# A windowed-attention layer with its projections issued as two 64-column matmuls each

## The chip, the cores and the metric

One core of a Trainium2 chip runs the whole kernel. The metric is the device time of one execution in microseconds (us), the median of a few runs; the profile is of one further execution. The engines are named as the profile names them: PE (TensorE, with PEld for its weight loads), DVE (VectorE), ACT (ScalarE), POOL (GpSimd), SP (SyncE, which here issues the DMAs).

## What is computed

The input is x, 16 images of 56 x 56 positions with 384 channels, fp32. It is group-normalised (32 groups), then goes through shifted-window attention with 7 x 7 windows (49 tokens) and 12 heads of 32, and is added to x:

```python
xn = _gn(x)                                    # 32 groups per image
xr = jnp.roll(xn, shift=(-3, -3), axis=(1, 2))
q, k, v = jnp.split(xr @ w_qkv.T, 3, axis=-1)  # cut in 7x7 windows, 12 heads
dots = einsum('bhwid,bhwjd->bhwij', q, k) * 32 ** -0.5
dots = dots + pos_emb[rel[:, :, 0], rel[:, :, 1]] + mask
out = einsum('bhwij,bhwjd->bhwid', softmax(dots), v)
out = out @ w_out.T + b_out
return x + jnp.roll(out, shift=(3, 3), axis=(1, 2))
```

## The kernel before

Most fp32 operands are split in an fp16 high part and an fp16 low part, and a product is then three matmuls: high x high, high x low, low x high.

The work goes by rows of windows. A row has eight windows, taken as four pairs. In most tiles a pair's first window has partitions 0 to 48 and its second 64 to 112. A *tick* (class `Tick`) covers two rows, so it has eight *steps*, k = 0 to 7, one for each pair. There are 64 ticks (4 per image) and 512 steps, numbered t. The program of a step is written out by hand for each engine (the functions `step`), and all engines meet through counting semaphores. Steps 4 to 7 repeat the pattern of 0 to 3 for the other row; "first to fourth step" below means k = 0 to 3 or k = 4 to 7.

In one step PE does, in this order (`step` of the tensor block):

- scores of t: 24 matmuls of 49 columns, one for each head and window, out to `ps_sa` (line 1121, in the helper `score_blocks`); the two windows of a head come one after the other and go to partitions 0 and 64
- `transpose_attended` of t-3: three full-width fp32 transposes of `av` (line 1172)
- the first part of the step's *units*
- `attend` of t-2: 36 matmuls with 33 or 32 moving columns (lines 1163 to 1165)
- the second part of the units
- `transposed_scores` of t-1: for each half of the heads a bias matmul of 294 moving columns (line 1150) and 12 score matmuls added onto it (line 1121)
- `project_out` of t-3: nine matmuls of 384 moving columns (line 1181)
- `shift_rows` of t: two matmuls of 49 moving columns (line 1139), which bring the row maxima to the transposed side
- the third part of the units

A unit fills one of two PSUM banks with part of the projections for the next row: q or k (line 1087, nine matmuls of 392 moving columns), v (line 1083, nine of 384), or x (line 1071, four fp32 transposes of newly loaded input). The table `FILL` says which units stand in which part of which step; in the fourth step the second part is empty. In 15 ticks the statistics of the next image add two small units.

DVE's order in a step: `lg` (scores plus bias, line 900), `mx` (row maxima, 911), low part of the first unit (`vl` 860, `qk` 865; `xn` 852 for x), `atl` of t-3 (low part of the attended rows, 907), the maxima by window `mw` (917) and their high and low part `mt` (928, 932), `rv` and `av` of t-2 (936, 941), the second units, statistics of a slab (`st`, 701), the output `xb` of t-3 (947), the low part `pl` of half the probabilities (953), the third units. ACT makes the high parts: `ath` of t-3 (653) first, then the first units, `xh` (605), the second units, the exponentials `pf` and `ph` of t-1 (664, 669), `tq` (658), the third units. POOL makes `xl` (529), the residual `xb` (537), the other half of `pl` (554), and `rb` (575).

The waits that matter below: `project_out` waits for `atl`; `atl` for `ath`; `ath` for the attended transposes; these for `av` of their step and for the output of the step before; `shift_rows` for the second `mt`; POOL's `xl` for `xh`; a unit for DVE's low part of the unit two before it; `av` of t-2 for the transposes of t-3.

## Time and profile before

| | us |
|---|---|
| median of 3 runs (4583.33 to 4587.28) | 4586.78 |
| the profiled execution | 4584.81 |
| its span, first to last instruction | 4583.0 |
| PE busy | 4390.2 (96 %) |
| DVE busy | 4046.9 (88 %) |
| ACT busy | 2275.8 (50 %) |
| POOL busy | 2282.0 (50 %) |

The granted TensorE clock is 0.998 over the span. Busy shares of PE are of matmuls as the profile models them: their ends overlap, so pace is read from starts. The page's largest groups on PE are the three of line 1087 (2304 matmuls each), of line 1083 and of line 1181 (1536 each).

### The profile page before, as it was taken

Reading aid. Unit: us, or ns where it says so; the run is one execution under the profiler, and the core shown is the slowest. Engines: PE = TensorE matmul, PEld = TensorE weight load, DVE = VectorE, ACT = ScalarE, POOL = GpSimd, SP = SyncE. Lnnn points to the kernel's source line nnn. Section 1 sums busy time; section 2 is a strip of 40 time slices with the busy share of each in tenths; the row PEclk is TensorE's granted clock in tenths of the full one; section 3 lists DMA queues with packets and bytes.
Section 4 is the critical chain, followed back from the end, with each engine's and each line's share of the span. In section 5 each row is a group of like instructions: output and inputs, shape, how many; then the busy total and the mean of one; then the engine's idle time right before and its main releaser. Section 6 shows DMA issues by size and latency. Waiting matters only on the chain.

```text
span 4583.0 us, 164167 instructions
## 1 busy us (share of the span) xinstructions
PE 4390.2 (96%) x64360; PEld 2981.1 (65%) x64360; DVE 4046.9 (88%) x9283; ACT 2275.8 (50%) x4225; POOL 2282.0 (50%) x1933
## 2 busy tenths in 40 slices
PE   3999999999999999999999999999999999999998
PEld 1666666666666666666666666666666666666665
DVE  5898898989989998898989989899898988999886
ACT  0555555455554545555555455555555555555554
POOL 1455445455554554555455455545545545554454
PEclk9999999999999999999999999999999999999999
DMA  4344344334343433443343443334434433434332
GB/s 122 103 106 107 99 107 116 94 108 114 99 109 105 108 104 103 107 109 98 105 119 95 108 112 100 107 106 108 105 97 109 115 95 107 115 98 108 98 95 60
DMA packets 231099, 478.93 MB, mean 105 GB/s; under 512 B 39009, under 2 KB 140898, under 8 KB 222818
## 3 DMA queue, kind: packets, MB, share of 16 engines
q1 hardware_dynamic: 230338, 468.43, 38.6%
q8 instruction: 521, 8.54, 0.8%
q14 instruction: 240, 1.97, 0.1%
HBM read 159.99 MB, written 77.07 MB: 52 GB/s over the span
## 4 chain that ended last, share of the span: by engine, by line
PE 74%; DVE 16%; issue 7%; ACT 2%; SPq 0%; DMA 0%; POOL 0%; DVEq 0%; POOLq 0%; ACTq 0%
PE ps_pj L1087 24%; PE ps_pj L1083 13%; PE ps_post L1181 13%; PE ps_post L1172 5%; PE ps_sa L1121 4%; PE ps_st L1121 3%; PE ps_pv L1165 2%; DVE mt L928 2%; PE ps_st L1150 2%; PE ps_pv L1164 2%; PE ps_pv L1163 2%; DVE atl L907 2%; DVE mw L917 2%; PE ps_pj L1071 2%; DVE st L701 1%
## 5 line engine op out<-in xcount | busy, mean ns | idle before, releaser
L554 POOL TENSOR_TENSOR pl<-pf,ph 64x588 f16<-64x588 f32 x512 | 732.1, 1430 | 1622.3 <-ACT ph L669 1595.0
L599 ACT ACTIVATE qk<-ps_pj 128x392 f16<-128x392 f32 x768 | 381.9, 497 | 978.7 <-PE ps_pj L1087 978.7
L669 ACT ACTIVATE ph<-ps_st,sc 64x588 f16<-64x588 f32 x1024 | 772.5, 754 | 6.5
L1087 PE MATMUL ps_pj<-xh,wh 128*128 128x392 f16 x2304 | 765.2, 332 | 5.5 <-POOL xl L529 4.6
L1087 PE MATMUL ps_pj<-xh,wl 128*128 128x392 f16 x2304 | 764.6, 332 | 0.0
L1087 PE MATMUL ps_pj<-xl,wh 128*128 128x392 f16 x2304 | 764.5, 332 | 0.0
L575 POOL TENSOR_TENSOR rb<-tq,cst 128x588 bf16<-128x588 bf16 x512 | 701.2, 1370 | 48.1 <-ACT tq L658 8.1
L529 POOL TENSOR_TENSOR xl<-xn,xh 128x392 f16<-128x392 f32 x384 | 343.4, 909 | 599.0 <-DVE vl L860 293.0
L865 DVE TENSOR_TENSOR qk<-ps_pj,qk 128x392 f16<-128x392 f32 x768 | 432.8, 564 | 228.3 <-ACT qk L599 225.4
L664 ACT ACTIVATE pf<-ps_st,sc 128x588 f32<-128x588 f32 x512 | 384.7, 751 | 359.1 <-PE ps_st L1121 359.1
L953 DVE TENSOR_TENSOR pl<-pf,ph 64x588 f16<-64x588 f32 x512 | 543.4, 1061 | 0.5 <-ACT ph L669 0.5
L1181 PE MATMUL ps_post<-woh,ath 128*98 128x384 f16 x1536 | 521.8, 340 | 18.6 <-DVE atl L907 11.0
L595 ACT ACTIVATE vh<-ps_pj 128x384 f16<-128x384 f32 x512 | 252.7, 494 | 546.4 <-PE ps_pj L1083 546.4
L1163 PE MATMUL ps_pv<-vh,ph 128*128 128x33 f16 x6144 | 516.3, 177 | 3.1 <-issue 2.8
L1165 PE MATMUL ps_pv<-vh,pl 128*128 128x33 f16 x6144 | 515.3, 177 | 0.0
L1164 PE MATMUL ps_pv<-vl,ph 128*128 128x32 f16 x6144 | 515.2, 177 | 0.0
L537 POOL TENSOR_TENSOR xb<-xs,bout 98x384 f32<-98x384 f32 x512 | 515.0, 1006 | 0.0
L1163 PEld LDWEIGHTS ps_pv<-vh,ph 128*128 128x128 f16 x6144 | 484.1, 96 | 39.6 <-issue 3.7
L1083 PE MATMUL ps_pj<-wh,xh 128*128 128x384 f16 x1536 | 501.0, 326 | 3.2 <-DVE qk L865 1.3
L1181 PE MATMUL ps_post<-wol,ath 128*98 128x384 f16 x1536 | 502.2, 327 | 0.0
L1181 PE MATMUL ps_post<-woh,atl 128*98 128x384 f16 x1536 | 502.1, 327 | 0.0
L1083 PE MATMUL ps_pj<-wh,xl 128*128 128x384 f16 x1536 | 500.3, 326 | 0.0
(107 smaller groups left out, 9582.0 us busy)
## 6 DMA issues: line engine op xcount, KB each, us to landing
stack<-qk SPq DMA_DIRECT2D x1536, 147.0 KB
sx<-in_x SPq DMA_DIRECT2D x66, 1176.0 KB, 7.0
xs<-in_x SPq DMA_DIRECT2D x384, 84.0 KB
out<-xb SPq DMA_DIRECT2D x384, 84.0 KB
xs<-in_x SPq DMA_DIRECT2D x384, 63.0 KB
out<-xb SPq DMA_DIRECT2D x384, 63.0 KB
xs<-in_x SPq DMA_DIRECT2D x128, 66.0 KB
out<-xb SPq DMA_DIRECT2D x128, 66.0 KB
```

Source lines behind the costliest of these rows:

```text
L537: nc.gpsimd.tensor_tensor(xb[:, j, :], xs[:, j // 4, j % 4, :], bout[:, :], ALU.add).then_inc(s_xb, 1)
L554: nc.gpsimd.tensor_tensor(pl[PAD:, :, PAD:PAD + N], pf[PAD:, :, :], ph[PAD:, :, PAD:PAD + N], ALU.subtract).then_inc(s_pl[1], 1)
L575: nc.gpsimd.tensor_tensor(rb[:, :, :, :], tq[:, :, :].unsqueeze(2).broadcast_to([128, 2, HH, N]), const_of("own_head").unsqueeze(1).unsque ...
L669: e = nc.scalar.activation(ph[rows, :, w * PAD:w * PAD + N].rearrange("p (a h) n -> p a h n", a=2), ps_st[rows, :, 0:HH * N].rearrange("p ...
L865: nc.vector.tensor_tensor(qk[:, lp, i, :], ps_pj[bank][:, 0:RT], qk[:, hp, i, :], ALU.subtract).then_inc(s_pjr, 1)
L953: nc.vector.tensor_tensor(pl[0:PAD, :, 0:N], pf[0:PAD, :, :], ph[0:PAD, :, 0:N], ALU.subtract).then_inc(s_pl[0], 1)
L1083: m = mm(ps_pj[bank][:, 0:C], xa[:, b, c, 2 * i:2 * i + 2, :].rearrange("p w n -> p (w n)"), wa[:, c, 2 * C:3 * C], **on)
L1087: m = mm(ps_pj[bank][:, 0:RT].rearrange("p (w n) -> p w n", w=NW), wa[:, c, o:o + 128], xa[:, b, c, :, 0:N], **on)
L1163: mm(out, ph[:, h, :], v, start=True, stop=False, skip_group_check=True)
L1164: mm(out[:, 0:HD], ph[:, h, :], vl[:, odd, p, h, :], start=False, stop=False, skip_group_check=True)
L1165: m = mm(out, pl[:, h, :], v, start=False, stop=True, skip_group_check=True)
L1181: m = mm(ps_post[0:PT, 0:C], a[:, c, :], w[:, c, :], start=c == 0 and n_ == 0, stop=c == KC - 1 and n_ == 2)
```

## The change

Each projection matmul, each output-projection matmul, each bias matmul and each shift-row matmul becomes two. Both read the same moving operand; the first has the stationary columns 0 to 63 and writes partitions 0 to 63, the second has the rest and writes from partition 64 (34 of them in the output projection, which has 98 columns). Attention (`attend`) and the fp32 transposes stay as they are.

The order changes too. On PE `transpose_attended` moves from behind the scores to behind `attend`. On ACT `ath` moves behind the first units. On DVE `atl` moves from ahead of the maxima to behind `av`. In `FILL` the units x0 and x1 change places with q2 and k2 of their part.

```diff
--- before.py
+++ after.py
@@ -23,6 +23,7 @@
 GC = C // GROUPS
 EPS = 1e-5
 TALL = WS - DISP
+SIDES = (slice(0, PAD), slice(PAD, 2 * PAD))
 BIG = 1e30
 
 
@@ -117,7 +118,7 @@
 
 
 FILL = [([("q", 0)], [("k", 0)], [("q", 1)]),
-        ([("k", 1)], [("q", 2), ("x", 0)], [("k", 2), ("x", 1)]),
+        ([("k", 1)], [("x", 0), ("q", 2)], [("x", 1), ("k", 2)]),
         ([("v", 0)], [("x", 2)], [("v", 1)]),
         ([("v", 2)], [], [("v", 3)])]
 ROW_UNITS = [u for parts in FILL for part in parts for u in part]
@@ -635,10 +636,11 @@
             def step(tk):
                 for k in range(8):
                     t = 8 * tk.n + k
+                    if not (tk.last and k >= 4):
+                        units(tk, k, 0)
                     if not (tk.first and k < 3):
                         attended_high(t - 3)
                     if not (tk.last and k >= 4):
-                        units(tk, k, 0)
                         x_highs(tk, k)
                         units(tk, k, 1)
                     if not (tk.first and k < 1):
@@ -973,8 +975,6 @@
                     maxima(t, k)
                     if not (tk.last and k >= 4):
                         units(tk, k, 0)
-                    if not (tk.first and k < 3):
-                        attended_low(t - 3)
                     if tk.finishes and k == 4:
                         dve.wait_ge(s_bn, SLABS + 2 + n)
                         stat_sums()
@@ -987,6 +987,8 @@
                         invert(t - 2)
                     if not (tk.first and k < 2):
                         normalize(t - 2)
+                    if not (tk.first and k < 3):
+                        attended_low(t - 3)
                     if not (tk.last and k >= 4):
                         units(tk, k, 1)
                     if tk.measures and k == 0:
@@ -1012,9 +1014,9 @@
             for m in range(B):
                 image(m)
             end = 8 * (LAST + 1)
-            attended_low(end - 3)
             invert(end - 2)
             normalize(end - 2)
+            attended_low(end - 3)
             output(end - 3, 5)
             split_probabilities(end - 1)
             attended_low(end - 2)
@@ -1079,13 +1081,14 @@
                 for c in range(KC):
                     for n_, (xa, wa) in enumerate(((xh, wh), (xh, wl), (xl, wh))):
                         on = dict(start=c == 0 and n_ == 0, stop=c == KC - 1 and n_ == 2)
-                        if kind == "v":
-                            m = mm(ps_pj[bank][:, 0:C], xa[:, b, c, 2 * i:2 * i + 2, :].rearrange("p w n -> p (w n)"),
-                                   wa[:, c, 2 * C:3 * C], **on)
-                        else:
-                            o = (C if kind == "k" else 0) + i * 128
-                            m = mm(ps_pj[bank][:, 0:RT].rearrange("p (w n) -> p w n", w=NW), wa[:, c, o:o + 128],
-                                   xa[:, b, c, :, 0:N], **on)
+                        for s, half in enumerate(SIDES):
+                            if kind == "v":
+                                m = mm(ps_pj[bank][half, 0:C], xa[:, b, c, 2 * i + s, :], wa[:, c, 2 * C:3 * C],
+                                       skip_group_check=True, **on)
+                            else:
+                                o = (C if kind == "k" else 0) + i * 128 + s * PAD
+                                m = mm(ps_pj[bank][half, 0:RT].rearrange("p (w n) -> p w n", w=NW), wa[:, c, o:o + PAD],
+                                       xa[:, b, c, :, 0:N], skip_group_check=True, **on)
                 m.then_inc(s_pj, 1)
 
             for c in range(KC):
@@ -1136,7 +1139,8 @@
                 pe.wait_ge(s_ml, t + 1)
                 need(pe, s_tc, t)
                 for hh in range(2):
-                    m = mm(rows_out[:, hh, :], mt[:, hh, :], eb[:, :], start=True, stop=True)
+                    for half in SIDES:
+                        m = mm(rows_out[half, hh, :], mt[:, hh, half], eb[:, :], start=True, stop=True)
                 m.then_inc(s_tp, 1)
 
             def transposed_scores(t, tk, k):
@@ -1146,9 +1150,9 @@
                 need(pe, s_ph, t)
                 kind = bias_kind(tk, odd, p)
                 for hh in range(2):
-                    out = ps_st[:, hh, 0:HH * N]
-                    mm(out, bt[:, kind, :], rb[:, hh, :, :].rearrange("p h n -> p (h n)"),
-                       start=True, stop=False, skip_group_check=True)
+                    for half in SIDES:
+                        mm(ps_st[half, hh, 0:HH * N], bt[:, kind, half], rb[:, hh, :, :].rearrange("p h n -> p (h n)"),
+                           start=True, stop=False, skip_group_check=True)
                     m = score_blocks(ps_st, odd, p, hh, True, start=False, stop=True, skip_group_check=True)
                 m.then_inc(s_st, 1)
 
@@ -1178,8 +1182,9 @@
                 pe.wait_ge(s_al, t + 1)
                 for c in range(KC):
                     for n_, (a, w) in enumerate(((ath, woh), (ath, wol), (atl, woh))):
-                        m = mm(ps_post[0:PT, 0:C], a[:, c, :], w[:, c, :], start=c == 0 and n_ == 0,
-                               stop=c == KC - 1 and n_ == 2)
+                        for part in (slice(0, PAD), slice(PAD, PT)):
+                            m = mm(ps_post[part, 0:C], a[:, c, part], w[:, c, :], start=c == 0 and n_ == 0,
+                                   stop=c == KC - 1 and n_ == 2, skip_group_check=True)
                 m.then_inc(s_out, 1)
 
             def back(tk, k, lag):
@@ -1189,12 +1194,12 @@
                 for k in range(8):
                     t = 8 * tk.n + k
                     scores(t, tk, k)
-                    if not (tk.first and k < 3):
-                        transpose_attended(t - 3, k - 3 + 8)
                     if not (tk.last and k >= 4):
                         units(tk, k, 0)
                     if not (tk.first and k < 2):
                         attend(t - 2, *back(tk, k, 2))
+                    if not (tk.first and k < 3):
+                        transpose_attended(t - 3, k - 3 + 8)
                     if not (tk.last and k >= 4):
                         units(tk, k, 1)
                     if not (tk.first and k < 1):
@@ -1215,8 +1220,8 @@
             for m in range(B):
                 image(m)
             end = 8 * (LAST + 1)
+            attend(end - 2, Tick(B - 1, PARTS - 1), 6)
             transpose_attended(end - 3, 5)
-            attend(end - 2, Tick(B - 1, PARTS - 1), 6)
             transposed_scores(end - 1, Tick(B - 1, PARTS - 1), 7)
             project_out(end - 3)
             transpose_attended(end - 2, 6)
```

Three places show the order. First PE in the third step (k = 2), from the x unit on: transposes of x, bias and scores, and the beginning of the output projection. Before:

```order
L1071 MATMUL ps_pj<-cst,xs 128x98 x4
L1150 MATMUL ps_st<-rb,bt 128x294
L1121 MATMUL ps_st<-stack 49x49 x12
L1150 MATMUL ps_st<-rb,bt 128x294
L1121 MATMUL ps_st<-stack 49x49 x12
L1181 MATMUL ps_post<-woh,ath 98x384
```

After, from the attended transposes on:

```order
L1176 MATMUL ps_post<-cst,av 128x128 x3
L1073 MATMUL ps_pj<-cst,xs 128x98 x4
L1154 MATMUL ps_st<-rb,bt 64x294 x2
L1124 MATMUL ps_st<-stack 49x49 x12
L1154 MATMUL ps_st<-rb,bt 64x294 x2
L1124 MATMUL ps_st<-stack 49x49 x12
L1186 MATMUL ps_post<-woh,ath 64x384
L1186 MATMUL ps_post<-woh,ath 34x384
```

The attended transposes (`av`) now stand next to those of x, and bias and output projection are in halves around the scores.

Second DVE in the same step, from the maxima to the output. Before:

```order
L911 TENSOR_REDUCE mx<-lg 128x12 [waits logits_made]
L860 TENSOR_TENSOR vl<-ps_pj,vh 128x384 [waits attended_in_psum,high_part_written]
L907 TENSOR_TENSOR atl<-ps_post,ath 128x294 [waits output_in_psum,attended_high]
L917 TENSOR_TENSOR mw<-mx,cst 128x24 [waits maxima_made]
L928 CAST mt<-mw 128x2x12 [waits shift_rows_in_psum,maxima_by_window]
L932 TENSOR_TENSOR mt<-mw,mt 128x2x12 [waits maxima_high]
L936 RECIPROCAL rv<-ps_pv 128x12 [waits attended_in_psum]
L941 TENSOR_TENSOR av<-ps_pv,rv 128x384 [waits attended_transposed,sums_inverted]
L852 TENSOR_SCALAR xn<-ps_pj,coef 128x392 [waits x_low_written,x_high_written,unit_in_psum]
```

After:

```order
L913 TENSOR_REDUCE mx<-lg 128x12 [waits logits_made]
L862 TENSOR_TENSOR vl<-ps_pj,vh 128x384 [waits attended_in_psum,high_part_written]
L919 TENSOR_TENSOR mw<-mx,cst 128x24 [waits maxima_made]
L930 CAST mt<-mw 128x2x12 [waits shift_rows_in_psum,maxima_by_window]
L934 TENSOR_TENSOR mt<-mw,mt 128x2x12 [waits maxima_high]
L938 RECIPROCAL rv<-ps_pv 128x12 [waits attended_in_psum]
L943 TENSOR_TENSOR av<-ps_pv,rv 128x384 [waits attended_transposed,sums_inverted]
L909 TENSOR_TENSOR atl<-ps_post,ath 128x294 [waits output_in_psum,attended_high]
L854 TENSOR_SCALAR xn<-ps_pj,coef 128x392 [waits x_low_written,x_high_written,unit_in_psum]
```

`atl` moved from behind the unit's low part to behind `av`.

Third ACT in the same step. Before:

```order
L653 ACTIVATE ath<-ps_post 128x294
L595 ACTIVATE vh<-ps_pj 128x12x32
L605 ACTIVATE xh<-xn 128x8x49 x2
L664 ACTIVATE pf<-ps_st,sc 128x588
L669 ACTIVATE ph<-ps_st,sc 64x12x49 x2
```

After:

```order
L596 ACTIVATE vh<-ps_pj 128x12x32
L655 ACTIVATE ath<-ps_post 128x294
L606 ACTIVATE xh<-xn 128x8x49 x2
L666 ACTIVATE pf<-ps_st,sc 128x588
L671 ACTIVATE ph<-ps_st,sc 64x12x49 x2
```

`ath` moved behind the unit's high part `vh` and stays ahead of `xh`.

## Rows read from the trace of the kernel before

**Rows 1.** Busy time by stretch: us, busy PE, PEld, DVE, ACT, POOL, clock, DMA; k 0-3, 7

```profile
2061.54:2070.48 8.94, 8.94 (x128) 5.91 (x127) 8.55 (x27) 4.32 (x8) 3.67 (x4) 1.00 0.16 51
2070.48:2080.12 9.64, 9.64 (x137) 6.70 (x137) 8.86 (x24) 4.56 (x9) 4.17 (x4) 1.00 0.16 51
2080.12:2088.38 8.26, 7.98 (x125) 5.38 (x124) 7.65 (x16) 4.54 (x9) 5.66 (x6) 1.00 0.67 162
2088.38:2096.44 8.06, 7.42 (x121) 5.11 (x120) 7.92 (x21) 4.35 (x8) 4.04 (x5) 1.00 0.43 100
2123.27:2130.76 7.49, 7.49 (x119) 5.11 (x118) 7.35 (x14) 4.35 (x8) 4.74 (x5) 1.00 0.53 123
```

**Rows 2.** Timeline of PE, a second step: start, us to the last end, work

```profile
2001.00 0.33 PE L1087 MATMUL ps_pj<-xl,wh 128*128 128x392 f16 x1
2001.26 0.50 PE L1121 MATMUL ps_sa<-stack 96*49 96x49 f16 x24
2001.69 0.55 PE L1172 MATMUL ps_post<-cst,av 128*128 128x128 f32 x3
2002.07 0.33 PE L1087 MATMUL ps_pj<-xh,wh 128*128 128x392 f16 x1
...
2003.61 0.18 PE L1163 MATMUL ps_pv<-vh,ph 128*128 128x33 f16 x1
...
2004.51 0.33 PE L1087 MATMUL ps_pj<-xh,wh 128*128 128x392 f16 x1
```

**Rows 3.** Timeline of PE in the same step, transposed scores

```profile
2006.38 0.29 PE L1150 MATMUL ps_st<-rb,bt 128*128 128x294 bf16 x1
2006.60 0.34 PE L1121 MATMUL ps_st<-stack 96*49 96x49 f16 x12
2006.87 0.30 PE L1150 MATMUL ps_st<-rb,bt 128*128 128x294 bf16 x1
```

**Rows 4.** Groups by line: weight loads of the output projection, busy us, mean ns

```profile
L1181 PEld LDWEIGHTS ps_post<-woh,atl 128*98 128x98 f16 x1536 | 191.1, 124 | 59.8
```

**Rows 5.** Timeline of PE, a fourth step: attended transposes and first unit

```profile
2089.39 0.52 PE L1172 MATMUL ps_post<-cst,av 128*128 128x128 f32 x3 [0.52 <-DVE xb L947]
2089.75 0.33 PE L1083 MATMUL ps_pj<-wh,xh 128*128 128x384 f16 x1
...
2091.05 0.33 PE L1083 MATMUL ps_pj<-wh,xl 128*128 128x384 f16 x1
```

**Rows 6.** Timeline, a third step: first unit's last matmul, then DVE

```profile
2082.34 0.33 PE L1083 MATMUL ps_pj<-wh,xl 128*128 128x384 f16 x1
...
2083.23 0.56 DVE L860 TENSOR_TENSOR vl<-ps_pj,vh 128x384 f16<-128x384 f32 x1 [0.19 <-ACT vh L595]
2083.71 0.45 DVE L907 TENSOR_TENSOR atl<-ps_post,ath 128x294 f16<-128x294 f32 x1
2084.08 0.77 DVE L917 TENSOR_TENSOR mw<-mx,cst 128x24 f32<-128x24 f32 x1
2084.88 0.82 DVE L928 CAST mt<-mw 128x24 bf16<-128x24 f32 x1
2085.74 0.93 DVE L932 TENSOR_TENSOR mt<-mw,mt 128x24 bf16<-128x24 f32 x1
```

**Rows 7.** Timeline of DVE, the second step ahead of it

```profile
2074.45 0.17 DVE L917 TENSOR_TENSOR mw<-mx,cst 128x24 f32<-128x24 f32 x1
...
2074.97 0.23 DVE L936 RECIPROCAL rv<-ps_pv 128x12 f32<-128x12 f32 x1
2075.23 0.56 DVE L941 TENSOR_TENSOR av<-ps_pv,rv 128x384 f32<-128x384 f32 x1
```

**Rows 8.** Timeline of ACT and POOL in the third step of rows 6

```profile
2083.23 0.96 ACT L605 ACTIVATE xh<-xn 128x392 f16<-128x392 f32 x2
2083.90 1.77 POOL L529 TENSOR_TENSOR xl<-xn,xh 128x392 f16<-128x392 f32 x2 [1.83 <-DVE vl L860]
2085.62 0.99 POOL L537 TENSOR_TENSOR xb<-xs,bout 98x384 f32<-98x384 f32 x1
```

## The prediction

> **What bounds the kernel now.** I read first the view of busy time by stretch, over four steps in a row [rows 1]. In the first two steps of each four TensorE (PE) is busy in every slice: 8.94 of 8.94 and 9.64 of 9.64 us. In the third and fourth it waits: 7.98 of 8.26 and 7.42 of 8.06. The eighth step of a tick is the fourth again, but at 7.49 us without that wait. A tick is thus 2 x (8.94 + 9.64 + 8.26) + 8.06 + 7.49 = 69.2 us, and 64 ticks make 4430 of the 4583 us span. VectorE (DVE) is nearly as full: 8.55, 8.86, 7.65, 7.92. So PE is the bound with DVE close behind it, and each PE gain must be followed into DVE.
>
> The PE timeline [rows 2] gives the prices. A projection of nine 392-column matmuls takes 1.54 us from its first start to the next group's, 0.171 each; the 384-column ones start 0.163 apart (eight of them in 1.30 [rows 5]). From the last of a projection to the scores it is 0.26, that is 0.09 more. The 24 score matmuls then take 0.43 us to the next start: the last starts 0.50 - 0.187 = 0.31 in, so 0.12 passes there where 0.03 would do, again 0.09 more. The 36 attention matmuls take 0.90. In the transposed scores [rows 3] the full-width bias matmul of 294 columns is followed only after 0.22 us (at the pace of the projections 294 columns are 0.13) and the 12 score matmuls by 0.27, of which 0.15 is from their first start to their last. Each place where the output width goes from 128 to 64 columns, or back, costs some 0.09 us: the next group starts only when the one before has left the array. There are six such places in a step: into and out of the scores, and four in the transposed scores.
>
> **The change part by part.** *Switches.* With projections, output projection, bias and shift rows in halves, the order of a step becomes: scores, first units, bias, output projection, shift rows and last units at 64 wide; attention and the transposes of attended rows stand together at 128. That leaves two switches. An x transpose is still full-width: x2 stands next to the attended transposes, and x0 too, now ahead of q2, at no cost; x1 stands alone between shift rows and k2 and costs two. So four switches go in steps 0, 2, 3 and two in step 1: 0.36, 0.18, 0.36, 0.36, or 1.26 us per four steps, 128 x 1.26 = 161 us in all.
>
> *The halves themselves.* A tick has 180 full-width matmuls in its 20 projection units and 72 in its output projections; 64 x 252 = 16,128 pairs take their place. If the halves run side by side, a pair takes the time of one. The trace has no such pair of 384 columns; the nearest rows are the scores, which are issued in such pairs (window 0 to partitions 0 to 48, window 1 to 64 up). 24 of them start within 0.31 us, 0.027 per pair, where one after the other 49 columns each would need at least 2 x 0.020 at the 2.4 GHz of the rows (granted clock 1.00). So they overlap. Their excess over one stream is 0.007 per pair; the full-width 392-column matmul with the same 49-column blocks has the same excess (0.170 against 0.163). I take zero per pair. The upper end is 0.005 more for the 9216 pairs of 384 columns, +46 us; a gain is excluded, since a pair streams as many columns as the matmul it replaces.
>
> Weight loads double in number. A 98-column load is 0.124 us long [rows 4] and already hidden under the output projection's 0.163; two shorter ones, side by side as in the scores, I cost at nothing. The cover is the stream of the matmul before; without it each pair would pay some 0.1 us. The Trainium skill speaks against the change here: its page TensorEngine Tiling (Array Packing), section on feature incompatibilities, says that column tiling cannot be combined with the fast weight load. By that rule the projections' loads get longer. The trace's 98-column loads, 0.124 us under a pace of 0.163, agree that a longer load can stay under cover; the sum would be the same by both while loads run ahead, and 1600 us more (0.1 per pair) if in halves they could not.
>
> *The new place of the attended transposes and of atl.* Before, PE transposed the attended rows of three steps back right after the scores, and DVE made atl (the low half of them) ahead of the maxima. Now PE does it after the attention matmuls, ScalarE (ACT) makes ath after the first unit's high part, and DVE makes atl after mw, mt, mt, rv and av. PE's transposes no longer wait for the previous step's output: the 0.52 us of [rows 5] in the fourth step goes. But the output projection, which waits for atl, now has that whole chain ahead of it, and with it everything behind it on PE: shift rows, last units, the next scores.
>
> I walk the fourth step, from its first score. PE: scores 0.34, unit 1.47, switch 0.09, attention 0.90, transposes 0.38, switch 0.09, transposed scores 0.62 (0.98, twice the 0.49 of [rows 3], less four switches): output projection possible at 3.89. DVE: its low part of the first unit starts 0.73 after the unit's last column (2082.34 + 0.16 to 2083.23 [rows 6]), that is at 1.81 + 0.73 = 2.54. Then from start to start: vl 0.48 [rows 6]; mw, mt and mt together 0.52, rv 0.26, av 0.56 less the 0.08 by which the next operation overlaps [rows 7]; atl 0.45 and 0.05 for the semaphore: 4.78. PE waits 0.9 us. After it come output projection 1.47, shift rows 0.05, unit 1.47: 7.77. DVE enters such a step some 0.1 late, so I take 7.9. In the third step the x transpose fills 0.34 of the same wait and the end is the same, 7.9 (it was 8.26). In steps 0 and 1 a unit of 1.53 stands between transposes and output projection, and the wait is covered: 8.58 and 9.46.
>
> This walk uses short mw and mt. In the third step now they take 0.77, 0.82 and 0.93 [rows 6] instead of 0.17 each ([rows 7]); each ends as an operation of GpSimd (POOL) does: xl, xl, xb end at 2084.8, 2085.7 and 2086.6 [rows 8]. DVE's small SBUF operations stand still while POOL has one in progress. In the changed order ath waits for transposes that end at 3.3 in the step, and xh comes behind it at about 3.8 instead of 3.1, so xl moves from 3.8 to about 4.5; DVE, without atl ahead, has done its maxima from 3.0 to 3.6. They miss each other by some 0.9 us.
>
> *Statistics.* Fifteen ticks carry the statistics: their two full-width units add four switches (0.36), and small DVE steps among the maxima now stand ahead of atl, about 0.4 in each of two steps. 15 x 1.2 = 18 us.
>
> *Sum.* Tick: 2 x (8.58 + 9.46 + 7.9 + 7.9) = 67.7, 1.5 less than 69.2; 64 x 1.5 = 98; less 18 is 80. In terms of the edit, 161 us of switches go, and waits for atl eat half of it, net of the waits that vanish. The profiled execution took 4584.8 us, two below the median of 4586.8: 4585 - 80 = 4505; with the DVE entry at its early value (7.77 for the third and fourth step) it is 4472. I take 4495, nearer to the late end, because DVE is that full.
>
> **Rivals.** *A, PE waits no more than now.* If the chain to atl is as short as the gaps, all 161 us come out: 4424. For it: DVE loses blocked time in two steps. Against it: the 0.9 us are a chain of dependences, not of load. Without the waits that show as idle PE now (2 x 0.28 + 0.64 per tick) it would be 77 us lower still, 4350.
>
> *B, POOL still hits the maxima, slower.* The place is the third and fourth step: if DVE comes 0.9 us later than in my walk, or xl earlier, mw, mt, mt are stretched by 2.0 and 0.8 us as now, and this time the output projection waits behind them. That adds 2.8 us per four steps: 128 x 2.8 = 358, some 4850. It decides from 0.7 us per four steps on, about one blocked operation. For it: DVE is over 90 % busy. Against it: each time PE waits for atl, DVE gains on it, so DVE can't stay late.
>
> *C, the halves don't overlap over long streams.* 16,128 x 0.163 = +2630 us, about 7100. Only the scores speak on this, and they speak against it, with streams of 49 columns. With 0.005 per pair it is +46, some 4540; the skill's page TensorE: Matmul & The Clock Gate, section on the measured speedup of packing, puts about 4 ns on each further tile, and taken per pair that would be an estimate of +65 us, 4560.
>
> **How the numbers follow.** My forecast with its sizes uncertain (4450 to 4560) 0.60; A 0.20 (0.05 of it below 4400); B 0.14, of which 0.04 ends near no change and 0.10 slower; C in full 0.03; the rest, 0.03, is slower by something not seen. A difference of 0.2 % (9 us) is about what a measurement can tell from none. Faster 0.81, same 0.04, slower 0.15. The range that leaves out no more than 0.2: 4400 to 4590.
>
> **What would show it.** Pairs start 0.17 and 0.163 apart and their halves within 0.01; the step from scores to unit and back costs no 0.09; busy PE in steps 0 and 1 with 8.6 and 9.5 us. In the third and fourth step the first output-projection matmul waits 0.5 and 0.9 us for DVE's atl, and mw and mt are near 0.2. If mt is at 0.8 there, B holds; if the output projection doesn't wait, A; if pairs take 0.2 or more, the price of the halves was wrong.

## Result and the profile after

The changed kernel takes 4662.34 us (median of 4 runs, 4661.47 to 4677.66) beside 4585.94 for the kernel before on the same chip: a ratio of 1.0175, 95 % interval 1.0154 to 1.0197. It is 76 us slower where the prediction had it some 90 us faster. The profiled execution took 4661.99 us, its span is 4660.2.

Busy time by stretch of the kernel after: us, busy PE, PEld, DVE, ACT, POOL, granted clock, DMA. The rows are a first step, a second (k = 5), a third and a fourth; then the sixth and the eighth step (k = 5, 7) of a tick with statistics, and a piece of that eighth step.

```profile
2093.84:2102.39 8.55, 8.55 (x172) 6.15 (x168) 7.55 (x27) 4.31 (x8) 3.02 (x4) 1.00 0.18 55
2067.93:2077.99 10.06, 9.66 (x178) 6.99 (x175) 7.25 (x16) 4.31 (x8) 4.39 (x4) 1.00 0.59 164
2043.53:2051.46 7.93, 7.37 (x156) 5.68 (x154) 6.58 (x19) 4.66 (x9) 5.22 (x6) 1.00 0.61 152
2051.46:2059.38 7.92, 7.04 (x153) 5.32 (x150) 6.25 (x18) 4.23 (x8) 5.64 (x5) 1.00 0.49 119
2277.26:2289.62 12.36, 9.88 (x179) 7.20 (x177) 10.88 (x23) 4.31 (x8) 5.15 (x5) 1.00 0.46 134
2297.86:2309.17 11.31, 8.64 (x154) 6.19 (x150) 8.18 (x20) 4.23 (x8) 6.22 (x6) 0.85 0.30 67
2304.56:2307.60 3.04, 3.04 (x24) 1.96 (x26) 0.11 (x1) 0.00 (x0) 1.24 (x1) 0.50 0.02 5
```

The first, third and fourth step are shorter than in [rows 1] and near the lengths that the walk gave. The second is 10.06 us long, where the walk had 9.46. The last three rows are what the prediction priced at 1.2 us per tick.

The table collects all steps of a kernel. A step runs from the first score matmul to that of the next step; each value is the median over the ticks without statistics (us; called ordinary below). The last two columns are the mean length of an ordinary tick (49 of 64; the first and the last are left out of the mean) and of one with statistics (15). Kernels further down are the experiments.

| kernel | k=0 | 1 | 2 | 3 | 5 | 7 | tick | statistics tick |
|---|---|---|---|---|---|---|---|---|
| before | 8.95 | 9.63 | 8.26 | 8.06 | 9.63 | 7.50 | 69.2 | 71.7 |
| predicted | 8.58 | 9.46 | 7.9 | 7.9 | 9.46 | 7.9 | 67.7 | 71.4 |
| after | 8.55 | 10.15 | 7.92 | 7.92 | 10.19 | 7.92 | 69.3 | 76.0 |
| e2, x ahead of q and k only | 8.95 | 10.43 | 8.14 | 8.05 | 10.46 | 7.50 | 70.6 | 75.1 |
| e3, halves only | 8.78 | 9.93 | 8.18 | 8.19 | 9.93 | 7.55 | 69.6 | 72.8 |
| e4, order only | 8.94 | 9.62 | 8.47 | 7.98 | 9.62 | 7.98 | 70.0 | 76.3 |
| e1, x behind q and k | 8.54 | 9.71 | 8.24 | 7.93 | 9.71 | 7.93 | 68.9 | 76.7 |
| e7, x0 behind q2 | 8.55 | 9.73 | 7.93 | 7.93 | 9.73 | 7.93 | 68.3 | 76.2 |
| e9, early load | 8.55 | 9.72 | 7.93 | 7.93 | 9.47 | 7.93 | 68.0 | 75.1 |
| e5, atl behind mt | 8.55 | 10.86 | 7.33 | 7.48 | 10.95 | 7.35 | 68.9 | 72.0 |
| e12, both | 8.55 | 9.71 | 7.33 | 7.47 | 9.46 | 7.35 | 65.8 | 70.7 |

**The halves.** PE timeline of the kernel after, a fourth step, from the attended transposes to the output projection (start, us to the last end, work; "x2" is the pair of halves):

```profile
2054.27 0.53 PE L1176 MATMUL ps_post<-cst,av 128*128 128x128 f32 x3
2054.72 0.32 PE L1154 MATMUL ps_st<-rb,bt 128*64 128x294 bf16 x2
2054.87 0.32 PE L1124 MATMUL ps_st<-stack 96*49 96x49 f16 x12
2055.04 0.29 PE L1154 MATMUL ps_st<-rb,bt 128*64 128x294 bf16 x2
2055.16 0.32 PE L1124 MATMUL ps_st<-stack 96*49 96x49 f16 x12
2056.37 0.35 PE L1186 MATMUL ps_post<-woh,ath 128*64 128x384 f16 x2 [0.89 <-DVE atl L909]
2056.55 0.34 PE L1186 MATMUL ps_post<-wol,ath 128*34 128x384 f16 x2
2056.71 0.34 PE L1186 MATMUL ps_post<-woh,atl 128*34 128x384 f16 x2
```

Behind the first one, which starts 0.18 ahead of the next, pairs start 0.16 apart, as single matmuls did in [rows 5]. Over the whole trace the usual distance from pair to pair is 0.163 us with 384 columns and 0.170 with 392, and the two halves of a pair mostly start 0.01 apart or less: a half costs nothing beside its twin. Behind a bias matmul the scores come after 0.12 to 0.15 us, not 0.22, and the next bias matmul 0.17 after them, not 0.27 [rows 3]. The output projection waits 0.89 us for `atl`; the prediction said 0.9.

**The maxima.** DVE timeline of the kernel after, the third step that began at 2043.53:

```profile
2046.69 0.18 DVE L919 TENSOR_TENSOR mw<-mx,cst 128x24 f32<-128x24 f32 x1
2046.90 0.18 DVE L930 CAST mt<-mw 128x24 bf16<-128x24 f32 x1
2047.11 0.19 DVE L934 TENSOR_TENSOR mt<-mw,mt 128x24 bf16<-128x24 f32 x1
...
2047.95 0.45 DVE L909 TENSOR_TENSOR atl<-ps_post,ath 128x294 f16<-128x294 f32 x1
```

Where 0.77, 0.82 and 0.93 us stood [rows 6] there are now 0.18, 0.18 and 0.19. POOL's `xl` begins at 2048.01, 0.8 us behind the last of them (predicted 0.9):

```profile
2048.01 1.77 POOL L530 TENSOR_TENSOR xl<-xn,xh 128x392 f16<-128x392 f32 x2 [2.50 <-ACT xh L606]
```

So far the prediction holds, in ordinary steps. Two things in it do not.

**First, x0.** The chain of waits of the kernel after, one second step that began at 2241.39 (of a statistics tick; at 10.62 us it is longer than the median of 10.15); then two rows of timelines, the first of SP's queue and the second of PE:

```profile
2242.23 0.83 SPq L401
2243.06 0.05 issue
2243.11 2.52 DMA xs<-in_x
2245.63 0.14 issue
2245.77 0.53 PE ps_pj L1073 x4
```

```profile
2235.66 8.19 SPq L401 DMA_DIRECT2D xs<-in_x  x10
```

```profile
2245.77 0.53 PE L1073 MATMUL ps_pj<-cst,xs 98*128 98x98 f32 x4 [0.98 <-DMA xs<-in_x]
```

Unit x0 transposes newly loaded rows. SP may issue their ten DMAs only when POOL has made the residual from the buffer for all four pairs, 2.8 us into the first step; it is busy with them for 8.2 us from 2235.66 on, and the landing that x0 waits for is at 2245.63, 12.8 us after the first step's start at 2232.84. Ahead of q2, PE is ready for x0 at 12.0 (2245.77 less the 0.98 us of waiting, counted from 2232.84). Behind q2, where it stood, it is due 1.5 us later, and the rows are there: the kernel before lists no wait of PE for them.

**Second, the statistics.** Timelines of the kernel after in the eighth step (k = 7) of a statistics tick, which began at 2297.86. DVE, and behind it POOL and PE:

```profile
2300.18 0.76 DVE L902 TENSOR_TENSOR lg<-ps_sa,bc 128x588 f32<-128x588 f32 x1
...
2302.42 0.89 DVE L825 SCALAR_TENSOR_TENSOR rs<-rs 128x32 f32<-128x32 f32 x1
...
2304.06 0.45 DVE L909 TENSOR_TENSOR atl<-ps_post,ath 128x294 f16<-128x294 f32 x1
```

```profile
2302.35 0.92 POOL L530 TENSOR_TENSOR xl<-xn,xh 128x392 f16<-128x392 f32 x1 [2.37 <-DVE vl L862]
```

```profile
2304.56 0.53 PE L1186 MATMUL ps_post<-woh,ath 128*64 128x384 f16 x2 [2.67 <-DVE atl L909]
2304.87 0.55 PE L1186 MATMUL ps_post<-wol,ath 128*34 128x384 f16 x2
2305.19 0.55 PE L1186 MATMUL ps_post<-woh,atl 128*34 128x384 f16 x2
```

DVE begins `lg` 2.3 us into the step, not 1.2 as in ordinary ones (2044.75 in the step that began at 2043.53). Then a statistics step `rs`, 0.19 us when alone, meets `xl` and takes 0.89. `atl`, last in that chain, is 1.8 us later in the step than usual, and the output projection waits 2.67 us. After that wait PE runs at a granted clock of 0.50, the lower of its two levels: pairs start 0.32 apart, not 0.16, through all nine of the output projection and two or three more. All 15 statistics ticks have this wait (2.67 us in 14 of them, 3.54 in one). In 13 the clock fell; in the first two it stayed at 1.00, behind the same wait, and there the step is 9.71 us long instead of 11.1 to 11.4. So the wait costs the 1.8 us by which it is longer, and the clock 1.4 to 1.7 more where it falls. The Trainium skill, page TensorE: Matmul & The Clock Gate, section on what is actually happening, has these two levels, half and full; the rows of 2304.56 (0.50) and of the steps around it (1.00) agree.

The same tick's sixth step (k = 5) has two more waits, PE timeline:

```profile
2282.60 0.36 PE L1090 MATMUL ps_pj<-xh,wh 128*64 128x392 f16 x2 [1.55 <-DVE qk L867]
...
2288.06 0.36 PE L1090 MATMUL ps_pj<-xh,wh 128*64 128x392 f16 x2 [0.93 <-DVE varb L808]
```

They fall on q2 and k2, each right behind a short x unit. A unit may start when DVE has cleared the unit two before it. With x0 behind q2 the long unit gives DVE 1.5 us for that; with x0 ahead DVE has the 0.4 us of the transposes. The step as a whole does not hang on that alone: in e7 below, with x0 back behind q2, this wait is gone, but waits of 1.32 us for `varb` and 0.78 for `atl` take its place, and the step is 12.67 us long instead of 12.36.

### The profile page after: what moved, and what is told of

Same layout as the page of the kernel before. It is cut to its first block, busy times and chain, and to the rows that moved or that the text cites. A ratio compares the mean times of both kernels' runs of the same rounds, so it can differ in the third digit from the quotient of the medians.

```text
span 4660.2 us, 200519 instructions
## 1 busy us (share of the span) xinstructions
PE 4234.7 (91%) x82536; PEld 3131.1 (67%) x82536; DVE 3678.3 (79%) x9283; ACT 2243.1 (48%) x4225; POOL 2338.6 (50%) x1933
## 3 DMA queue, kind: packets, MB, share of 16 engines
q1 hardware_dynamic: 230338, 468.43, 37.9%
q8 instruction: 663, 10.86, 1.0%
## 4 chain that ended last, share of the span: by engine, by line
PE 41%; DVE 18%; issue 12%; SPq 12%; ACT 6%; POOL 5%; DMA 5%; POOLq 0%; ACTq 0%; DVEq 0%
PE ps_pj L1090 13%; PE ps_post L1186 12%; SPq L401 11%; PE ps_pj L1086 8%; DMA xs<-in_x 4%; DVE lg L902 3%; DVE qk L867 3%; POOL rb L576 3%; PE ps_pj L1073 2%; ACT ph L671 2%; DVE atl L909 2%; ACT qk L600 2%; POOL xb L538 2%; DVE pl L955 2%; DVE st L703 1%
## 5 line engine op out<-in xcount | busy, mean ns | idle before, releaser
L555 POOL TENSOR_TENSOR pl<-pf,ph 64x588 f16<-64x588 f32 x512 | 796.0, 1555 | 1543.5 <-ACT ph L671 1499.6
L1090 PE MATMUL ps_pj<-xh,wh 128*64 128x392 f16 x4608 | 793.8, 338 | 47.2 <-DVE qk L867 28.5
L1090 PE MATMUL ps_pj<-xh,wl 128*64 128x392 f16 x4608 | 782.1, 333 | 0.0
L1090 PE MATMUL ps_pj<-xl,wh 128*64 128x392 f16 x4608 | 781.8, 333 | 0.0
L1186 PE MATMUL ps_post<-woh,ath 128*64 128x384 f16 (+1 forms) x3072 | 525.1, 334 | 225.4 <-DVE atl L909 225.4
L949 DVE SCALAR_TENSOR_TENSOR xb<-ps_post,sc,xb 98x384 f32<-98x384 f32 x512 | 313.3, 612 | 367.0 <-PE ps_post L1186 367.0
L1186 PE MATMUL ps_post<-woh,atl 128*64 128x384 f16 (+1 forms) x3072 | 521.6, 332 | 0.0
L1186 PE MATMUL ps_post<-wol,ath 128*64 128x384 f16 (+1 forms) x3072 | 521.4, 331 | 0.0
L1086 PE MATMUL ps_pj<-wh,xh 128*64 128x384 f16 x3072 | 516.5, 328 | 1.2 <-DVE vl L862 0.7
L1086 PE MATMUL ps_pj<-wl,xh 128*64 128x384 f16 x3072 | 514.1, 327 | 0.9 <-issue 0.9
```

The source lines that it names most:

```text
L555: nc.gpsimd.tensor_tensor(pl[PAD:, :, PAD:PAD + N], pf[PAD:, :, :], ph[PAD:, :, PAD:PAD + N], ALU.subtract).then_inc(s_pl[1], 1)
L1086: m = mm(ps_pj[bank][half, 0:C], xa[:, b, c, 2 * i + s, :], wa[:, c, 2 * C:3 * C], skip_group_check=True, **on)
L1090: m = mm(ps_pj[bank][half, 0:RT].rearrange("p (w n) -> p w n", w=NW), wa[:, c, o:o + PAD], xa[:, b, c, :, 0:N], skip_group_check=True, **on)
L1186: m = mm(ps_post[part, 0:C], a[:, c, part], w[:, c, :], start=c == 0 and n_ == 0, stop=c == KC - 1 and n_ == 2, skip_group_check=True)
```

## Experiments

### One part alone

**Only FILL back (e1).** The changed kernel with x0 and x1 behind q2 and k2 again:

```diff
-        ([("k", 1)], [("x", 0), ("q", 2)], [("x", 1), ("k", 2)]),
+        ([("k", 1)], [("q", 2), ("x", 0)], [("k", 2), ("x", 1)]),
```

> The changed kernel with one edit: x0 and x1 stand behind q2 and k2 again, as in the kernel before. Theory 1 (the new place of x0 and x1 is where the forecast gain went: x0 waits for the DMA of its input rows, and in statistics ticks q2 and k2 wait for banks): the second step falls from 10.2 us to about 9.64 although it has two more width switches, 128 x 0.55 = 70 us, and the statistics ticks lose another 2 to 3 us each, 40 us: about 4550 us. Rival (the waits come from the new order of transposes and atl, and the place of x does not matter): 4640 to 4670.

Measured: 4649.44 us, ratio 1.0135 (1.012 to 1.015). A miss, and a time within the rival's range. The second step fell from 10.15 to 9.71, but the third rose from 7.92 to 8.24: with x1 last in the second step, v0 must wait for a bank (PE's waits for `qk` ahead of v: 38.7 us, 127 times). And the statistics tick did not fall (76.7). So the place of x is one part, and another was still to be found.

**Only FILL swapped (e2)**: that line the other way round, in the kernel before.

> The kernel before with x0 and x1 ahead of q2 and k2, nothing else. Theory 1: the x0 transposes come some 0.3 us before their input has landed in every second step, 128 x 0.3 = 38 us, and statistics ticks lose 1 to 2 us: about 4640 us. Rival (the place of x does not matter): 4586 us within 10.

Measured: 4706.25, ratio 1.0259 (1.0244 to 1.0274). That is 66 us above the 4640 of the theory and far from the rival. The second step rises by 0.8 us and the statistics tick by 3.4, without halves and with the old order on DVE. The list of waits shows it: PE's waits by what is waited for, us in total, times, longest. The first row is new; the second stood at 37.9 before and is no part of the change.

```profile
PE ps_pj L1071 <- DMA xs<-in_x: 68.8, 107, 1.3
PE ps_post L1172 <- DVE xb L947: 38.1, 77, 0.8
```

**Only halves (e3)**: the changed kernel with the order of before on PE, DVE and ACT and in `FILL`; what is left of the diff is `SIDES` and the pairs of matmuls.

> Only the halves: the order of all engines is that of the kernel before. Width switches: four instead of six in steps 0, 2, 3 and eight instead of six in step 1, so 0.36 us less per four steps, of which the waits of the third and fourth step for DVE take some. Theory 1 (a pair of halves costs what one matmul did): 4540 to 4590 us, about 4565. Rival (halves cost time of their own, 0.005 us a pair or more): 4600 us or more.

Measured: 4619.77, ratio 1.007 (1.0055 to 1.0085). The whole is a miss and lies in the range of the rival, that halves cost time of their own. But pairs start 0.163 and 0.170 us apart here too, so it is not they. The first step is as expected: 8.95 to 8.78, two switches fewer at 0.085 each. In the second step the order of before leaves x0 and x1 alone between halves and costs eight switches instead of six: +0.30, where two at 0.09 would be 0.18. The fourth is 0.13 longer; PE's waits for the second `mt` add up to 75.5 us in this kernel, 37.0 in the kernel before. So halves alone, in this order, lose 32 us.

**Only the order (e4)**: the kernel before with the new order of `transpose_attended`, `ath` and `atl`; full-width matmuls and the old `FILL`.

> Only the order: attended transposes behind attention, ath behind the first units, atl behind av; full-width matmuls, x behind q2 and k2. By the walk of the prediction the third and fourth step come to 7.9 us each instead of 8.26 and 8.06 (7.49), first and second stay: -31 us; statistics ticks lose 2 to 4 us each as atl now stands behind DVE's statistics steps, +30 to 60. Theory 1: 4585 to 4620, about 4600. Rival (the order alone explains the slowdown): 4660 or more.

Measured: 4698.29, ratio 1.0245 (1.0228 to 1.0262). A miss, in the rival's range (the order alone explains the slowdown). The eighth step goes from 7.50 to 7.98, the third from 8.26 to 8.47, and the statistics tick from 71.7 to 76.3. So most of the surcharge of the statistics comes with the order, not with the halves: a statistics tick is 2.5 us longer than an ordinary one in the kernel before, 3.1 with halves alone, 4.5 with the new place of x alone, 6.2 with the order alone, 6.8 in the changed kernel.

### The place of x0

**x0 behind q2, x1 ahead of k2 (e7):**

```diff
-        ([("k", 1)], [("x", 0), ("q", 2)], [("x", 1), ("k", 2)]),
+        ([("k", 1)], [("q", 2), ("x", 0)], [("x", 1), ("k", 2)]),
```

> The changed kernel with one edit: x0 stands behind q2 again, x1 stays ahead of k2. Theory 1 (x0 comes before the DMA of its rows has landed; x1 in its new place is a gain, since it frees the bank for the next step's first unit): second step 9.65 us instead of 10.15, third step stays 7.92, so 68.2 us a tick without statistics: about 4580 to 4600 us. Rival (both places cost): 4640 or more.

Measured: 4614.45, ratio 1.0067 (1.0052 to 1.0082); an ordinary tick is 68.3 instead of 69.3 (expected 68.2). The whole is 14 us above the expected range, since a statistics tick stays at 76.2. x1's new place is a gain (4649.44 in e1 against this), x0's a loss of 48 us.

**Early load (e9).** Was it x0's place, or that its rows come late? SP issues each pair's loads when that pair's residual is made, instead of all after the fourth:

```diff
-                        reach(s_xb, 8 * n + 4 * odd + 4)
...
-                        load_row(ahead(tk), odd)
+                        for q in range(PAIRS):
+                            reach(s_xb, 8 * n + 4 * odd + 1 + q)
+                            move_row(sp, x, xs[:, odd, q, :], s_load[odd], q, True, rows_of(ahead(tk), odd))
```

> The changed kernel with one edit: SP issues the input loads of each of the four pairs as soon as that pair's residual is made, instead of all ten DMAs after the fourth. Six of ten DMAs can go out 1 to 1.5 us earlier, and the last lands earlier by as much. Theory 1 (x0 waits for its input): the second step falls from 10.15 to about 9.5 us, 128 x 0.6 = 77 us: 4580 to 4600 us. Rival (x0 waits for something else, a bank or the order on PE): 4655 to 4665.

Measured: 4589.88 (10 runs), ratio 1.0013 (1.0004 to 1.0022). x0 keeps its place and its wait is gone: in the kernel after its transposes were idle 54.0 us for the DMA (77 times); here no wait for it is listed. The sixth step is 9.47, the 9.46 of the walk. The second stays at 9.72; there PE waits 0.19 us for DVE's `qk`. (Of the 38.8 us in the second row below, 12 are these; 24 are the wait of 1.61 in the sixth step of the 15 statistics ticks.) The slab statistics stand in the first four steps of a tick only, which would explain it, but was not tried. Waits of PE in this kernel:

```profile
PE ps_post L1187 <- DVE atl L910: 226.9, 274, 2.7
PE ps_pj L1091 <- DVE qk L868: 38.8, 77, 1.6
```

The first row is what is left, and it is as large as in the kernel after (225.4, 273 times).

### The place of atl

**atl right behind the second mt (e5)**, ahead of `rv` and `av`, all else as changed:

```diff
                     maxima_low(t)
+                    if not (tk.first and k < 3):
+                        attended_low(t - 3)
...
                         normalize(t - 2)
-                    if not (tk.first and k < 3):
-                        attended_low(t - 3)
```

> The changed kernel with one edit: DVE makes atl ahead of rv and av (behind the maxima) instead of behind them. Theory 1 (in the third and fourth step PE waits for the chain low part, maxima, rv, av, atl): atl ends 0.65 us earlier, the third and fourth step fall from 7.92 to about 7.3 us each, 4 x 0.6 x 64 = 150 us: 4500 to 4530 us. Rival (the third and fourth step are bound by DVE's whole load, not by the place of atl): no more than 20 us gained, 4640 to 4665.

Measured: 4574.16 (10 runs), ratio 0.9981 (0.9969 to 0.9993). Above the expected 4500 to 4530. Third and fourth step fell to 7.33 and 7.48 as expected, but in an ordinary tick most of that (1.8 of 2.2 us by the means) was given back in the second steps, 10.86 and 10.95 in the median. What is left is mostly in the statistics ticks: 76.0 to 72.0 us, 60 of the 82 us between the two profiled executions; their eighth step falls from 11.32 to 7.72. Waits of PE:

```profile
PE ps_pj L1073 <- DMA xs<-in_x: 149.1, 122, 2.0
PE ps_post L1186 <- DVE atl L909: 49.7, 138, 1.0
```

The wait for `atl` went from 225 us to 50, and that for x0's rows from 54 to 149. PE arrives sooner at a transfer that doesn't come sooner. This is why each cure alone seemed weak.

**Both (e12)**: e5 and e9 together.

> The changed kernel with both edits that gained: atl ahead of rv and av, and each pair's input loads issued when its residual is made. Theory (two separate waits: the chain to atl in the third and fourth step, and the landing of the input in the second; shortening the first made the second longer, 10.15 to 10.8 us): second step 9.5 to 9.7, third and fourth 7.3 to 7.5, 65.8 us a tick without statistics: 4380 to 4410 us. Rival (a common bound such as the DMA queue or DVE's load holds the rate): no better than 4500.

Measured: 4413.26, ratio 0.9623 (0.9607 to 0.9639), 3 us above the expected range and the fastest of the kernels that leave nothing out: 3.8 % below the kernel before, 5.3 % below the changed one. Alone e9 gives 72 us and e5 88, together they give 249. In an ordinary tick the early load alone gives 1.3 us, `atl` first alone 0.3, both 3.5. Busy time by stretch, of a sixth, a third and a fourth step, then of the sixth step of a statistics tick:

```profile
2231.42:2240.88 9.46, 9.46 (x177) 7.01 (x175) 7.33 (x16) 4.32 (x8) 4.39 (x4) 1.00 0.54 160
2208.06:2215.40 7.34, 7.34 (x156) 5.70 (x154) 6.09 (x18) 4.66 (x9) 4.65 (x5) 1.00 0.66 165
2215.40:2222.87 7.47, 7.08 (x153) 5.33 (x151) 6.86 (x19) 4.24 (x8) 5.66 (x5) 1.00 0.53 128
2429.14:2443.29 14.15, 11.43 (x179) 8.20 (x177) 11.15 (x23) 4.32 (x8) 5.44 (x5) 0.88 0.39 112
```

PE is busy all through the first two rows; the fourth step still waits 0.4 us. The last row is the statistics again. No run has this order with full-width matmuls, so how much of the 249 us needs the halves was not measured.

**Transposes first (e6, e10, e11).** Another cure of the same wait: on PE the attended transposes ahead of `attend`, on DVE `atl` at its place of before, x0 behind q2 (e6); the same with the early load (e10); and with x0 ahead of q2 (e11). The part of e6's edit on PE:

```diff
+                    if not (tk.first and k < 3):
+                        transpose_attended(t - 3, k - 3 + 8)
                     if not (tk.first and k < 2):
                         attend(t - 2, *back(tk, k, 2))
-                    if not (tk.first and k < 3):
-                        transpose_attended(t - 3, k - 3 + 8)
```

> Halves as in the changed kernel, but on PE the attended transposes stand ahead of attention instead of behind it (still next to it, so no further width switch), atl is at its old place on DVE ahead of the maxima, and x0 stands behind q2. Theory: atl is ready before PE has done the transposed scores, so the third step falls to 7.3 and the fourth to 7.0 us, second 9.7: 65.1 us a tick: 4330 to 4360 us, and no window of half clock in the statistics ticks. Rival (DVE's load or POOL's hold on it takes the gain back, mw and mt long again as in the kernel before): 4450 to 4550.

> The kernel of the run before it with the early input loads. Theory: with x0 behind q2 the input lands in time, so the loads no longer matter: within 20 us of that kernel. Rival (shorter third and fourth steps make the loads late again, since SP issues them one after another): 40 us or more better than it.

> The same with x0 ahead of q2 as in the changed kernel: two width switches fewer in the second step, 128 x 0.18 = 23 us less, if the early loads have landed by then; if they haven't, x0 waits 0.3 us or more in each second step and this kernel is slower than the one with x0 behind q2 by 20 to 60 us. I expect the latter by a little, since the faster third and fourth steps bring x0 nearer to its loads.

Measured: 4424.27 (0.9647, 0.9632 to 0.9661), 4425.97 (0.965, 0.9635 to 0.9664) and 4423.95 (0.9647, 0.9632 to 0.9661). An ordinary tick is 65.8 us in all three, as in e12. e6 is a miss, 64 us above its range: an ordinary tick was expected at 65.1, and its statistics tick is 71.9 us, 6.1 more than an ordinary one, 15 times, 92 us. It was expected to be free of the half clock, and is not: 11 of the 15 sixth steps have it. e10 is as expected. In e11 the two switches fewer were to give 23 us or late rows to cost 20 to 60; it is neither: the second steps are 9.72 and 9.59 instead of 9.73 and 9.73. With the rows there in time the place of x0 costs next to nothing, and gains next to nothing.

### The statistics

**Out of the maxima chain (e8).** The two statistics steps between `mw` and the second `mt` moved behind `atl`:

```diff
                     maxima_by_window(t, k)
-                    between(5)
                     maxima_high(t)
-                    between(5)
                     maxima_low(t)
...
                         attended_low(t - 3)
+                    between(5)
+                    between(5)
```

> The changed kernel with one edit: DVE's small statistics steps, which stood between mw, mt and mt in 15 ticks, come behind atl. Theory 1 (a statistics tick costs 6.7 us more than another, against 2.5 in the kernel before, because POOL holds up a statistics step and the wait for atl then gets so long that the TensorE clock falls to half): the surcharge falls to 3 to 4 us, 15 x 3 = 45 us: about 4615 to 4630, granted clock back to 0.997. Rival (the surcharge comes from the widths and places of the statistics units on PE): 4655 to 4665.

Measured: 4658.64, ratio 1.0164 (1.0149 to 1.0179), a miss: 75.9 us a tick. The time is the rival's, widths and places of the statistics units on PE; but the widths are not it, as e4 has the surcharge with full-width matmuls. Their places on PE were not varied. The two moved steps are two of six; the others stand ahead of the next `lg`. PE's wait for `atl` in the eighth step is 2.58 us instead of 2.67.

**The two large ones cut (e13).** At the end of the fifth step two operations of 1.0 us each, `dev` and its square, stand ahead of `lg`:

```diff
-                    ins = nc.vector.tensor_tensor(dev2[:, :, :, :], dev[:, :, :, :], dev[:, :, :, :], ALU.mult)
+                    ins = nc.vector.tensor_tensor(dev2[:, 0:n], dev[:, 0:n], dev[:, 0:n], ALU.mult)
```

(`n` is 1 slab of 4, and likewise for `dev`; the kernel leaves out three quarters of that part of the variance.)

> The changed kernel, with the two large statistics operations of DVE (dev and its square, 1.02 us each, at the end of the fifth step of 15 ticks, ahead of the next step's lg) cut to one slab of four, 64 of 256 columns; three quarters of that part of the variance is left out. A statistics tick of the changed kernel lasts 76.0 us against 69.3 of the others. Theory: these two make DVE late for the sixth step and the lateness is handed on as a wait for a bank there and as the 2.7 us wait for atl in the eighth step; without about 1.5 us of it the statistics ticks fall by 3 us or more, 15 x 3 = 45 us, so 4600 to 4630. Rival: the damage is from the small steps inside the maxima chain of the sixth to eighth step; then only the 1.5 us themselves go, at most 22 us, 4640 to 4660.

Measured: 4648.22, ratio 1.0143 (1.0128 to 1.0158), and 75.3 us a tick. The sixth step falls by 0.45 us (12.36 to 11.91); the eighth stays at 11.37. The size is the rival's, but the test is weaker than it was meant to be. With a quarter of the columns `dev` takes 0.71 us instead of 1.03 and its square 0.93 instead of 1.06: each ends some 0.08 us behind the operation of POOL that was in progress (`rb`, `xb`). DVE is thus early by 0.46 us and not by 1.5, and PE's wait for `qk` in the sixth step falls by just that, from 1.61 to 1.16. So a lateness of DVE is handed on there one for one; the wait of 2.67 us in the eighth step does not move with it. What the two operations cost in full was not measured.

**All steps later (e14).** None at the end of the fifth step and none among the maxima; six in each of the last three steps, two behind `atl`, the rest around `xb` and at the end:

```diff
                         attended_low(t - 3)
+                    between(5)
+                    between(5)
...
-                    between()
-                    between()
+                    between(6)
+                    between(6)
```

> The changed kernel with all 18 statistics steps of DVE moved behind atl: none at the end of the fifth step and none among mw, mt, mt; in the sixth to eighth step they stand behind atl, around the output xb and at the end (six in each). No work is left out. Theory: the fifth step is back at 8.56 us, q2 of the sixth waits less and atl of the eighth is no longer late; against that the mean's steps end later and the var unit waits for them. Statistics ticks at 72 to 74 us instead of 76.0: 4605 to 4640. Rival: the steps cost the same wherever they stand: 4655 to 4665.

Measured: 4691.02, ratio 1.0236 (1.0219 to 1.0253), the wrong way. Both theories fall: the fifth step stays at 9.39, and the eighth rises to 13.45 us at a mean clock of 0.75 (11.3 and 0.85 in the kernel after), behind a wait for `atl` of 3.7 us:

```profile
2600.21:2613.66 13.45, 9.88 (x153) 6.70 (x149) 10.59 (x20) 4.23 (x8) 7.70 (x7) 0.75 0.30 74
```

**The same two on e12 (e15, e16).**

> The kernel with atl behind the second mt and early loads (4413 us), with the same cut as in the run with small dev: dev and its square on 64 of 256 columns, so part of the variance is left out. Its statistics ticks last 70.7 us against 65.8, and the sixth step alone 14.05 against 9.46. Theory: the 2.0 us wait of q2 for qk in the sixth step is this lateness; the ticks fall by 2 to 3 us: 4370 to 4385. Rival: at most the operations' own 1.5 us and less, since DVE has slack elsewhere: 4395 to 4413.

> The kernel with atl behind the second mt and early loads (4413 us), with the 18 statistics steps placed behind av and later, as in the run with the steps later; nothing is left out. Theory: statistics ticks at 68.5 to 70 us instead of 70.7: 4380 to 4405. Rival: the var unit waits for the later mean steps by as much as is gained: 4410 to 4420.

Measured: 4395.17 (0.959, 0.9575 to 0.9604) with the large ones cut, at the near end of the rival's range, and 4463.46 (0.9735, 0.972 to 0.975) with the steps later, which neither theory had. The first tells most. By the medians the sixth step falls from 14.05 to 12.12, by 1.9 us, though q2 waits only 0.46 less. PE timeline of e12:

```profile
2434.71 0.36 PE L1091 MATMUL ps_pj<-xh,wh 128*64 128x392 f16 x2 [1.83 <-DVE qk L868]
...
2435.62 0.54 PE L1091 MATMUL ps_pj<-xh,wl 128*64 128x392 f16 x2
```

and of e15, with the stretch of its whole step:

```profile
2425.16 0.36 PE L1091 MATMUL ps_pj<-xh,wh 128*64 128x392 f16 x2 [1.37 <-DVE qk L868]
```

```profile
2420.06:2432.18 12.12, 9.82 (x179) 7.23 (x177) 10.64 (x23) 4.32 (x8) 5.11 (x5) 1.00 0.44 130
```

In the first, pairs start 0.33 apart for some 3 us behind the wait, and the step's mean clock is 0.88; in the second it stays at 1.00. But it is not always so. The wait is 1.83 us in all 15 statistics ticks of e12: in 8 the clock fell and the step is 14.05 to 14.21 us long, in 7 it stayed and the step is 12.59. In e15 it is 1.37 in all 15: 12.12 us in 14 of them, and 13.74 in the one in which the clock fell. So where the clock falls it costs 1.5 to 1.6 us; by the means the step went from 13.42 to 12.23, and of these 1.2 us 0.46 are the wait and the rest is that the clock fell once and not eight times. 15 x 1.2 = 18 us, the whole difference between the two kernels. In e16 the eighth step shows the chain of the kernel after once more, this time with a cast of the maxima held up. DVE, PE, and a stretch of 3.4 us from the output projection on:

```profile
2487.11 0.91 DVE L931 CAST mt<-mw 128x24 bf16<-128x24 f32 x1
```

```profile
2488.66 0.35 PE L1189 MATMUL ps_post<-woh,ath 128*64 128x384 f16 x2 [2.98 <-DVE atl L910]
```

```profile
2489.00:2492.40 3.40, 3.40 (x30) 2.06 (x26) 1.84 (x6) 0.25 (x1) 0.93 (x2) 0.51 0.00 0
```

A cast that is 0.18 long elsewhere took 0.91 beside POOL's `xb` (2486.99, 0.99 long). So what the traces show in the eighth step is three things in a row: DVE enters the step late; a small operation then meets one of POOL; and behind the longer wait of PE the clock falls in most ticks, which doubles the distance from pair to pair for some 3 us. That the place of `atl` decides it is shown by e5 and e12: with `atl` ahead of `rv` and `av` the eighth step is at 7.72 instead of 11.32. How much of it each of the three causes is argued from the rows, except for the clock; no run takes away the meeting with POOL alone. Moving steps about moves the place of this, in e14 and e16 to a worse one. In the sixth step of e12, 8 falls of the clock are 12.5 us (8 steps against the 12.59 of the others); the shares of the rest stay open. 70.7 against 65.8 us, 15 times, is 74 us still lying there.

## Why the prediction was wrong

**Right.** The six places of 0.09 us: four fewer make the first step 0.40 shorter (predicted 0.36), two fewer 0.17 (e3, 0.18). The pairs cost nothing: 0.163 and 0.17 apart in all kernels with halves; rival C is out, and so is its milder form. The loads of 64 columns, 0.109 us long where those of 128 were 0.096, stay under cover. The Trainium skill's rule (TensorEngine Tiling (Array Packing), on feature incompatibilities) that column tiling excludes the fast weight load leaves no mark on that pace; and the 4 ns per further tile (TensorE: Matmul & The Clock Gate, on the measured speedup of packing), taken per pair, would by estimate have made 0.167 and 0.174 of it, which the rows do not show. The walk of third and fourth step gave 7.9 each, measured 7.92 and 7.92. Waits for `atl` of 0.5 and 0.9 us: 0.56 in the third step (its row of busy time: 7.93 less 7.37), 0.89 in the fourth. The maxima no longer meet `xl`, so rival B does not hold in ordinary ticks. (The prediction's listed chances add up to 0.80 for faster and 0.16 for slower, not to 0.81 and 0.15; nothing hangs on that.)

**Wrong, first step: "x0 too, now ahead of q2, at no cost".** I priced what x0 does to the array and not what it waits for. It stood behind 1.5 us of q2, and this was the cover of its transfer and of DVE's clearing of the bank. Two second steps per tick are 0.69 and 0.73 us too long; 1.4 us of the 1.57 by which an ordinary tick (69.27) exceeds the 67.7 of the sum. 49 x 1.57 = 77 us. e2, e7 and e9 show the cause from three sides: the loss comes with x0's new place alone, and goes with the old place or with earlier rows.

**Wrong, second step: the statistics at 1.2 us per tick.** The sum made them 67.7 + 2.5 (what they cost before) + 1.2 = 71.4; measured 76.0. 15 x 4.6 = 70 us. I counted the steps' own short durations ahead of `atl`, not that DVE came into them late, that one would meet POOL's `xl`, and that PE's wait would lower its clock. It is rival B's mechanism in 15 ticks of 64, with the clock on top: 15 falls of it (13 in the eighth step, 2 in the sixth) at some 1.6 us are 24 of the 70 us. The rest is DVE's lateness and the meetings with POOL; how it divides between them no run shows. B had its price from the maxima alone.

4505 by the sum + 77 + 70 = 4652, beside 4662 profiled. The remaining 10 are within first and last ticks and rounding; they were not looked for.

**Rival A** (4424, PE waits no more than now) did not come, but e12 and the e6 family show that it was to be had: with the chain to `atl` cut short and the rows there in time kernels with the same halves take 4413 to 4426. The argument against A was right that the chain is one of dependences; the order on DVE makes it.

## What to carry to other kernels

A unit that is moved to save the array something also moves its deadline: before pricing it at nothing, look up when its transfer lands and who clears its buffer, in each kind of step. Where a rare stretch (here 15 ticks of 64) loads an engine near its limit, walk that stretch by itself, with every short operation at its blocked length. And cures that each look weak may sit in series: the wait that one removes shows up at the next, so try them together before dropping either (here 72 and 88 us alone, 249 together). And a step that comes in two lengths has no typical one: count how often each occurs before reading a difference of medians (12.59 and 14.15 us in e12).
